# Gated linear attention between two expert layers: outputs in two parts, state copies on ScalarE, factors on GpSimd, a predicated mask, one table set

## The chip, the cores and the metric

The kernel runs on one core of one Trainium2 chip. The metric is the device time of one execution in microseconds, the lower the better; several executions give a median.

## What is computed

A block of three layers over x of 4096 tokens by 256: an expert layer at half weight, an attention layer, and the expert layer again with the same weights. Only the attention layer is touched. Cut to what matters:

```python
def step(S, qkva):                       # for each head, S is 64 x 64
    q_t, k_t, v_t, a_t = qkva
    S = a_t[..., None] * S + k_t[..., None] * v_t[..., None, :]
    o_t = jnp.einsum('bhk,bhkv->bhv', q_t, S)
    return (S, o_t)
# q, k, v = x @ W_q, x @ W_k, x @ W_v in 16 heads of 64; a = sigmoid(x @ W_gate + b_gate)
x = x + 0.5 * _L0_ffn_ref(_layernorm(x, axis=-1), ...)
x = x + _L0_attn_ref(_layernorm(x, axis=-1), W_q, W_k, W_v, W_gate, b_gate, W_o)
x = x + 0.5 * _L0_ffn_ref(_layernorm(x, axis=-1), ...)
```

## The kernel before

Each engine has a program of its own, and every hand-over between engines is a semaphore that the program names. `route` and `expert` are the expert layers; `attention()` on each engine is the stage in between.

**Tiling.** The tokens go in 8 supertiles of 4 tiles of 128 (`NSUP`, `SUPER`), the 16 heads in 8 pairs of two (`NPAIR`), so that a pair's 2 x 64 channels fill 128 partitions. The recurrence is written in chunks of 128 tokens: within a chunk a masked product of keys and queries (`scores`, `mask`), between chunks a state per pair that a scan carries on. Weights are fp32 split in two parts, and each projection (L616, L640, L698) is three passes over them.

**One pair, before the change.** A supertile is a loop body of 8 pairs; 7 supertiles run in a hardware loop and the last one follows it. For pair g of a supertile, with G = 8s + g:

- TensorE projects the gate of pair g+1 (`project_z`), turns the decayed keys (L650), takes the scores (L657), takes the outputs of pair g-1 (L683 from the state, L686 from the masked scores, alternating chunk by chunk), takes the additions to the state (L671, into bank 7), and projects q and k of pair g+1 (`project_qk`, L616).
- ScalarE makes Exp and Ln of the gates (L874, L876), copies the turned keys out of PSUM, makes the two decays with Exp (L883, L885), and rounds the outputs to their high part (`split_o`, by the helper at L757).
- VectorE does `chain` for pair g-1 (spread of the factors L1312, seed of the scan L1314, scan L1315, two spreads of the states into `state_in` L1319, copy-back L1321), sums the logs of pair g+1 (L1269), combines a token tile of the next supertile or takes its statistics, masks the scores (L1298, L1300, four pieces because one quarter of a chunk is never used), scales q and k of pair g+1 (`scaled`, L1277 to L1287, behind which `qk_made` rises), and takes the low part of the outputs of pair g-2 (`split_o`, L1326, behind which `ot_split` rises).
- GpSimd issues the indirect gathers of expert rows (L440), two for each token tile, each as soon as the tile's buffer is free.

**What sets the order.** The order on each engine is written out by hand in `supertile`; an engine waits in its own program order. `qd` is there twice, `prob`, `kd`, `state_in`, `factors`, `states` and each PSUM bank once, so the mask of pair g waits for the outputs of pair g-1 (`o_done`), and the outputs of g-1 wait for the chain of g-1 (`state_ready`) and the split of g-2 (`ot_split`). At the end of a supertile TensorE turns the next x, projects pair 0 of the next supertile, takes the last outputs, waits for their split, makes the output projection (L698) and the next values (`values`, L640, between which ScalarE makes Exp and Ln of the next pair 1), and goes round the loop.

## Time and profile before

| | us |
|---|---|
| median of 3 runs | 2530.24 |
| lowest, highest | 2522.37, 2537.93 |
| span of the profiled execution | 2566.5 |
| TensorE matmul busy in it | 2116.7 (82%) |
| VectorE busy | 1436.0 (56%) |
| ScalarE busy | 1187.6 (46%) |
| GpSimd busy | 263.8 (10%) |

The profiled execution is a single one of its own; of it the span from its first to its last instruction is recorded and no other time. The profile gives for each instruction its start and its duration, and for idle time in front of it what ended that. A matmul's end is modelled, so distances from start to start are the safer reading on TensorE. Matmuls of full fp32 appear as two instructions each.

### The profile page before, as it was taken

The page shows a single profiled execution, that of the slowest core. Times are in us where ns is not written, and L with a number is a line of the kernel's source. Part 1 is how long each engine was busy: PE and PEld are TensorE (multiplying, and loading weights), DVE is VectorE, ACT ScalarE, POOL GpSimd, SP SyncE. Part 2 cuts the span into 40 slices and gives each one's busy share as a digit, 9 for nine tenths or more (in the row PEclk, how much of TensorE's full clock was granted, in tenths as well). Part 3 has the DMA queues.
Part 4 walks back from the last instruction along what each step waited for, and adds up shares of the span by engine and source line. Part 5 has one row for each costly group of instructions (what it writes and reads, how often), then busy time and mean ns, then how long its engine had stood idle before and what let it go on. Part 6 is the DMA issues. An engine that isn't in the chain of part 4 may idle for free.

```text
span 2566.5 us, 39014 instructions
## 1 busy us (share of the span) xinstructions
PE 2116.7 (82%) x13967; PEld 1819.4 (71%) x13968; DVE 1436.0 (56%) x3544; ACT 1187.6 (46%) x1927; POOL 263.8 (10%) x268
## 2 busy tenths in 40 slices
PE   6079999999958897989888888985199999999780
PEld 5069889888856766666666666765088899988670
DVE  6345554555556675848494848556155545555442
ACT  1056655566535363535353544431166555666330
POOL 1700000000021010000000000003600000000324
PEclk9999999999979999989999999985599999999895
DMA  6322222222220000000000000001411221222214
GB/s 240 134 95 91 90 90 74 63 85 72 83 69 17 1 17 5 14 6 14 6 14 10 9 2 1 1 1 52 169 52 66 90 74 49 86 88 70 85 37 131
DMA packets 95432, 151.14 MB, mean 59 GB/s; under 512 B 9583, under 2 KB 76678, under 8 KB 94068
## 3 DMA queue, kind: packets, MB, share of 16 engines
q1 hardware_dynamic: 83008, 116.46, 13.4%
q0 software_dynamic: 12288, 32.91, 4.1%
q8 instruction: 81, 1.33, 0.2%
q14 instruction: 55, 0.45, 0.1%
HBM read 98.84 MB, written 51.15 MB: 58 GB/s over the span
## 4 chain that ended last, share of the span: by engine, by line
PE 55%; DVE 17%; issue 11%; PEld 7%; POOL 3%; ACT 3%; another core or an unknown queue 1%; SPq 1%; DMA 1%; PEldq 1%; DVEq 0%; POOLq 0%; ACTq 0%
PE bank L545 25%; PE bank L564 11%; PE bank L698 4%; PEld bank L564 3%; PEld bank L545 3%; PE bank L683 3%; PE bank L616 3%; PE bank L686 3%; PE bank L640 3%; DVE wide L1298 2%; DVE wide L1315 2%; DVE wide L1287 2%; DVE wide L1300 2%; DVE temp L1319 2%; DVE halves L1326 2%
## 5 line engine op out<-in xcount | busy, mean ns | idle before, releaser
L545 PE MATMUL bank<-halves 128*128 128x512 f32 (+2 forms) x3744 | 778.6, 368 | 35.5 <-DVE halves L1121 22.3
L545 PEld LDWEIGHTS bank<-halves 128*128 128x128 f32 x3744 | 654.0, 192 | 144.3 <-issue 28.3
L564 PE MATMUL bank<-halves 128*128 128x256 f32 (+1 forms) x3288 | 403.1, 283 | 3.0 <-issue 3.0
L564 PEld LDWEIGHTS bank<-halves 128*128 128x128 f32 (+1 forms) x3288 | 397.3, 189 | 5.7 <-issue 4.8
L801 ACT ACTIVATE temp<-bank,bias_now 128x512 f32<-128x512 f32 (+1 forms) x312 | 200.3, 642 | 389.0 <-PE bank L545 369.6
L1134 DVE SCALAR_TENSOR_TENSOR temp<-bank,bias_fc,temp 128x512 f32<-128x512 f32 (+1 forms) x312 | 216.1, 693 | 247.8 <-ACT temp L801 238.9
L616 PE MATMUL bank<-halves 128*128 128x512 f32 x1152 | 292.6, 406 | 2.0 <-DVE halves L1261 2.0
L1141 DVE TENSOR_TENSOR halves<-temp,halves 128x512 fp32r<-128x512 f32 (+1 forms) x312 | 198.1, 635 | 126.8 <-ACT halves L757 122.0
L616 PEld LDWEIGHTS bank<-halves 128*128 128x128 f32 x1152 | 217.0, 194 | 52.1 <-DVE halves L1261 2.4
L440 POOL DMA_INDIRECT halves<-expert_out,read_slot x96 | 102.9, 1072 | 1284.5 <-DMA expert_out<-rows 654.0
L757 ACT ACTIVATE halves<-temp 128x512 fp32r<-128x512 f32 (+1 forms) x313 | 184.9, 591 | 9.9
L1156 DVE TENSOR_TENSOR rows<-bank,rows 128x256 f32<-128x256 f32 (+1 forms) x160 | 66.8, 422 | 217.0 <-PE bank L564 191.0
L757 ACT ACTIVATE halves<-bank 128x512 fp32r<-128x512 f32 (+1 forms) x176 | 90.1, 545 | 211.4 <-PE bank L526 127.4
L808 ACT ACTIVATE temp<-temp 128x512 f32<-128x512 f32 (+1 forms) x312 | 179.9, 576 | 0.2
L683 PE MATMUL bank<-wide,temp 128*128 128x128 f32 x512 | 126.7, 330 | 63.9 <-DVE temp L1319 50.2
L433 POOL DMA_INDIRECT expert_in<-wide,temp x128 | 127.5, 996 | 422.1 <-DVE temp L1047 339.9
L757 ACT ACTIVATE halves<-wide 128x512 fp32r<-128x512 f32 (+1 forms) x196 | 115.5, 644 | 114.5 <-issue 96.5
L683 PEld LDWEIGHTS bank<-wide,temp 128*128 128x128 f32 x512 | 78.4, 193 | 110.1 <-issue 109.2
L1269 DVE TENSOR_TENSOR_SCAN wide<-wide,limit 128x64 f32<-128x64 f32 x512 | 101.0, 269 | 95.9 <-ACT wide L876 90.9
L526 PE MATMUL bank<-ident,wide 128*128 128x128 f32 x320 | 43.4, 276 | 122.6 <-DMA wide<-expert_in 122.6
L1298 DVE TENSOR_TENSOR wide<-bank,causal 64x512 f32<-64x512 f32 x128 | 87.3, 682 | 96.2 <-PE bank L657 54.7
L874 ACT ACTIVATE wide<-bank,bias_gate 128x512 f32<-128x512 f32 x64 | 44.0, 687 | 206.7 <-PE bank L616 183.3
(159 smaller groups left out, 2327.9 us busy)
## 6 DMA issues: line engine op xcount, KB each, us to landing
expert_out<-rows SPq DMA_DIRECT2D x144, 128.0 KB, 1.7
wide<-in_L_ffn_w_c_fc SPq DMA_DIRECT2D x16, 1024.0 KB
wide<-in_L_ffn_w_gate SPq DMA_DIRECT2D x16, 1024.0 KB
wide<-in_L_ffn_w_c_proj SPq DMA_DIRECT2D x16, 1024.0 KB
wide<-expert_in SPq DMA_DIRECT2D x32, 512.0 KB, 4.9
expert_in<-halves SPq DMA_DIRECT2D x9, 1024.0 KB
x<-in_L_attn_x SPq DMA_DIRECT2D x4, 1024.0 KB, 9.5
out_x<-x SPq DMA_DIRECT2D x32, 128.0 KB
```

Of the source, the lines that this page charges most:

```text
L433: pool.indirect_dma_start(expert_in, bass.IndirectOffsetOnAxis(ap=write_slot[:, j:j + 1], axis=0), xn[:, i, :], None, bounds_check=ROWS - ...
L440: pool.indirect_dma_start(into, None, expert_out, bass.IndirectOffsetOnAxis(ap=read_slot[:, j:j + 1], axis=0)).then_inc(landed, 16)
L545: m = pe.matmul(bank[at + b][:, 0:w], a[:, kc, j * P:(j + 1) * P], v[:, kc, 0:w], start=(i == 0), stop=(i == len(ps) - 1))
L564: mm = pe.matmul(bank[4 + t % 2][0:m, 0:C], a[:, j, o:o + m], v[:, j, :], start=(k == 0), stop=(k == len(ps) - 1))
L616: m = pe.matmul(bank[at][:], a[:, kc, g * P:(g + 1) * P], v[:, kc, :], start=(i == 0), stop=(i == len(ps) - 1))
L683: pe.matmul(bank[5][:, cols], state_in[:, c, :], qd[g % 2][:, c, :], start=True, stop=False, skip_group_check=True)
L757: return nc.scalar.activation(o, i, ACT.Copy)
L801: nc.scalar.activation(g_sb[b][:, 0:w], bank[2 + b][:, 0:w], ACT.Identity, bias=bias_now[:, j:j + 1]).then_inc(g_copied, 1)
L808: nc.scalar.activation(hg[b][:, 0:w], hg[b][:, 0:w], ACT.Silu).then_inc(silu_made, 1)
L1134: v.scalar_tensor_tensor(hg[b][:, 0:w], bank[b][:, 0:w], bias_fc[:, bass.ds(col, 1)], g_sb[b][:, 0:w], ALU.add, ALU.mult).then_inc(hg_made, 1)
L1141: v.tensor_tensor(s_lo[buf][:, j, 0:w], hg[b][:, 0:w], as_f32(s_hi[buf][:, j, 0:w]), ALU.subtract).then_inc(s_split, 1)
L1298: v.tensor_tensor(prob[h][lower, :, :], sc[lower, :, :], causal[lower, :].unsqueeze(1).to_broadcast([HALF, SUPER, P]), ALU.mult)
```

## The change

- **TensorE**: `scores` is cut in two, `turn_keys` and `scores`; `outputs` is cut in two, `outputs_of_state` (four products of the state, one behind the other) and `local_outputs` (eight products of the masked scores). For pair g the order is now turn_keys(g), outputs_of_state(g-1), scores(g), local_outputs(g-1), additions(g). `additions` waits for `state_seeded` in place of `state_kept`.
- **ScalarE**: it takes over the seed of the scan (`seed_states`), the two spreads and the copy-back (`spread_states`). One table set that holds Exp and Ln is loaded ahead of the stage.
- **GpSimd**: it takes over the spread of the factors (`spread_factors`), and its gathers are put in its program between these, one tile's in front of each of the first four pairs.
- **VectorE**: `mask` becomes a memset of one element and two predicated copies of whole blocks over buffers cleared once; `chain` is the scan alone, and is done for pair g right behind the mask of g, ahead of the split of g-1 and of `scaled` for g+1.

```diff
+                def spread_factors(s, g):
+                    G = s * NPAIR + g
+                    pool.wait_ge(qk_made, G + 1)
+                    if G:
+                        pool.wait_ge(state_summed, G)
+                    nc.gpsimd.tensor_copy(factors.rearrange("p (n c) -> p n c", n=DH),
+                                          carry[:, g % 2, :].unsqueeze(1).to_broadcast([P, DH, SUPER + 2])
+                                          ).then_inc(factors_made, 1)
...
+                    for b in range(SUPER):
+                        combine_from(b)
+                    for s in range(NSUP):
+                        for g in range(NPAIR):
+                            if s + 1 < NSUP and g < SUPER:
+                                combine_from((s + 1) * SUPER + g)
+                            spread_factors(s, g)
...
+                def outputs_of_state(s, g):
                     G = s * NPAIR + g
-                    pe.wait_ge(prob_made, G + 1)
                     if g:
                         pe.wait_ge(ot_split, G)
                     pe.wait_ge(state_ready, G + 1)
                     for c in range(SUPER):
-                        cols = slice(c * P, (c + 1) * P)
-                        pe.matmul(bank[5][:, cols], state_in[:, c, :], qd[g % 2][:, c, :],
-                                  start=True, stop=False, skip_group_check=True)
+                        pe.matmul(bank[5][:, c * P:(c + 1) * P], state_in[:, c, :], qd[g % 2][:, c, :],
+                                  start=(c == 0), stop=False, skip_group_check=True)
+
+                def local_outputs(s, g):
+                    pe.wait_ge(prob_made, s * NPAIR + g + 1)
+                    for c in range(SUPER):
                         for h in range(2):
-                            m = pe.matmul(bank[5][h * DH:(h + 1) * DH, cols],
+                            m = pe.matmul(bank[5][h * DH:(h + 1) * DH, c * P:(c + 1) * P],
                                           v_sb[:, c, g * P + h * DH:g * P + (h + 1) * DH], prob[h][:, c, :],
-                                          start=False, stop=True, skip_group_check=True)
+                                          start=False, stop=(c == SUPER - 1), skip_group_check=True)
                     m.then_inc(o_done, 1)
...
-                        scores(s, g)
+                        turn_keys(s, g)
                         if g + 1 == NPAIR and not last:
                             turn_x(s + 1)
+                        if g:
+                            outputs_of_state(s, g - 1)
+                        scores(s, g)
                         if g == 0:
                             project_qk(s, 1)
                         else:
-                            outputs(s, g - 1)
+                            local_outputs(s, g - 1)
                         additions(s, g)
...
+                def seed_states(s, g):
+                    G = s * NPAIR + g
+                    if g:
+                        act.wait_ge(state_summed, G)
+                    kv = bank[7][:, 0:DH * (SUPER + 2)].rearrange("p (n c) -> p n c", n=DH)
+                    copy(kv[:, :, 1], state[:, g, :]).then_inc(state_seeded, 1)
+
+                def spread_states(s, g):
+                    act.wait_ge(state_summed, s * NPAIR + g + 1)
+                    st = states.rearrange("p (n c) -> p n c", n=DH)
+                    for h in range(2):
+                        hp = slice(h * DH, (h + 1) * DH)
+                        i = copy(state_in[hp, :, hp].rearrange("p c n -> p n c"), st[hp, :, 1:SUPER + 1])
+                    i.then_inc(state_ready, 1)
+                    copy(state[:, g, :], st[:, :, SUPER + 1]).then_inc(state_kept, 1)
...
                         turned_keys(s, g)
+                        seed_states(s, g)
...
                         if g:
                             split_o(s, g - 1)
+                        spread_states(s, g)
...
+                nc.scalar.preload_act_table_set("natural_log_exp_and_others")
+                act.wait_ge(att_cleared, ATT_CLEARS)
...
-                    v.memset(prob[h][HALF:P, :, 0:HALF], 0.0).then_inc(att_cleared, 1)
+                    v.memset(prob[h], 0.0).then_inc(att_cleared, 1)
...
+                    v.memset(pause[:], 0.0)
                     for h in range(2):
                         sc = bank[3 + h][:].rearrange("p (a n) -> p a n", n=P)
-                        v.tensor_tensor(prob[h][lower, :, :], sc[lower, :, :],
-                                        causal[lower, :].unsqueeze(1).to_broadcast([HALF, SUPER, P]), ALU.mult)
-                        ins = v.tensor_tensor(prob[h][upper, :, upper], sc[upper, :, upper],
-                                              causal[upper, upper].unsqueeze(1).to_broadcast([HALF, SUPER, HALF]),
-                                              ALU.mult)
+                        ins = v.copy_predicated(prob[h], causal[:].bitcast(U16).unsqueeze(1).to_broadcast([P, SUPER, P]), sc)
                     ins.then_inc(prob_made, 1)
...
-                    dve.wait_ge(qk_made, G + 1)
-                    steps.after(v.tensor_copy(f, carry[:, g % 2, :].unsqueeze(1).to_broadcast([P, DH, SUPER + 2])))
+                    dve.wait_ge(factors_made, G + 1)
+                    if g:
+                        dve.wait_ge(state_kept, G)
                     dve.wait_ge(kv_done, G + 1)
-                    steps.after(v.tensor_copy(kv[:, :, 1], state[:, g, :]))
-                    steps.after(v.tensor_tensor_scan(states, bank[7][:, 0:DH * (SUPER + 2)], factors, 0.0,
-                                                     ALU.add, ALU.mult))
-                    for h in range(2):
-                        hp = slice(h * DH, (h + 1) * DH)
-                        ins = v.tensor_copy(state_in[hp, :, hp].rearrange("p c n -> p n c"), st[hp, :, 1:SUPER + 1])
-                    ins.then_inc(state_ready, 1)
-                    v.tensor_copy(state[:, g, :], st[:, :, SUPER + 1]).then_inc(state_kept, 1)
-                    dve.wait_ge(state_kept, G + 1)
+                    v.tensor_tensor_scan(states, bank[7][:, 0:DH * (SUPER + 2)], factors, 0.0,
+                                         ALU.add, ALU.mult).then_inc(state_summed, 1)
...
                     for g in range(NPAIR):
-                        if g:
-                            chain(s, g - 1)
...
                         mask(s, g)
+                        chain(s, g)
+                        if g:
+                            split_o(s, g - 1)
                         if g + 1 < NPAIR:
                             scaled(s, g + 1)
-                            if g:
-                                split_o(s, g - 1)
...
-                    chain(s, NPAIR - 1)
-                    split_o(s, NPAIR - 2)
```

## Rows read from the trace of the kernel before

**Rows 1.** Attention stage: length, busy PE PEld DVE ACT POOL, PEclk, DMA, GB/s
```profile
792.40:1718.50 926.10, 801.82 (x6033) 627.81 (x6033) 628.82 (x1898) 431.39 (x588) 45.38 (x48) 0.96 0.03 8
```

**Rows 2.** Timeline, TensorE, one pair: start, us, engine line operation [idle before]
```profile
1168.40 0.66 PE L650 MATMUL bank<-ident,wide 128*128 128x128 f32 x4
1168.98 1.16 PE L657 MATMUL bank<-wide 64*128 64x128 f32 x16
1171.42 0.46 PE L683 MATMUL bank<-wide,temp 128*128 128x128 f32 x2 [1.28 <-DVE temp L1319]
1171.81 0.44 PE L686 MATMUL bank<-wide 128*64 128x128 f32 x4
...
1174.44 0.64 PE L671 MATMUL bank<-wide,temp 128*64 128x64 f32 x16
...
1179.22 0.60 PE L650 MATMUL bank<-ident,wide 128*128 128x128 f32 x4
```

**Rows 3.** Timeline, VectorE, the same pair
```profile
1168.26 0.68 DVE L1326 TENSOR_TENSOR halves<-bank,halves 128x512 fp32r<-128x512 f32 x1
...
1171.64 1.78 DVE L1269 TENSOR_TENSOR_SCAN wide<-wide,limit 128x64 f32<-128x64 f32 x8
...
1174.73 0.68 DVE L1298 TENSOR_TENSOR wide<-bank,causal 64x512 f32<-64x512 f32 x1
...
1177.02 0.15 DVE L1277 COPY carry<-wide 128x1 f32<-128x1 f32 x1
...
1178.73 0.68 DVE L1326 TENSOR_TENSOR halves<-bank,halves 128x512 fp32r<-128x512 f32 x1
```

**Rows 4.** Chain of waits that ended last, 1168 to 1212 us, shares by line
```profile
by line: DVE wide L1287 10.7%; DVE wide L1298 9.3%; DVE wide L1315 8.8%; PE bank L683 8.5%; PE bank L686 7.7%; PE bank L616 7.6%; DVE temp L1319 7.0%; DVE halves L1326 6.8%; DVE wide L1269 6.6%; issue 6.6%; DVE wide L1300 5.8%; DVE temp L13
```

**Rows 5.** Timeline, TensorE, places in the first and the fifth supertile
```profile
797.05 0.69 PE L671 MATMUL bank<-wide,temp 128*64 128x64 f32 x16
...
799.16 0.60 PE L650 MATMUL bank<-ident,wide 128*128 128x128 f32 x4
...
1270.48 1.12 PE L650 MATMUL bank<-ident,wide 128*128 128x128 f32 x4 [5.28 <-issue]
...
1280.07 0.60 PE L650 MATMUL bank<-ident,wide 128*128 128x128 f32 x4
...
1343.07 0.66 PE L650 MATMUL bank<-ident,wide 128*128 128x128 f32 x4 [0.85 <-DVE wide L1287]
...
1344.74 1.09 PE L610 MATMUL bank<-ident,rows 128*128 128x128 f32 x8
...
1355.23 0.46 PE L683 MATMUL bank<-wide,temp 128*128 128x128 f32 x2 [1.15 <-DVE halves L1326]
...
1359.84 11.78 PE L698 MATMUL bank<-halves 128*128 128x256 f32 x96 [1.42 <-DVE halves L1326]
...
1383.50 1.65 PE L640 MATMUL bank<-halves 128*128 128x512 f32 x6 [0.97 <-ACT wide L757]
```

**Rows 6.** Groups by line: line engine op xcount | busy us, mean ns | idle before
```profile
L876 ACT ACT_TABLE_LOAD x64 | 82.1, 1283 | 1.2
L757 ACT ACTIVATE temp<-bank 128x512 f32<-128x512 f32 x80 | 46.0, 586 | 98.7 <-PE bank L650 77.2 <-PE bank L487 13.0 <-remote 8.5
L1315 DVE TENSOR_TENSOR_SCAN wide<-bank,temp 128x384 f32<-128x384 f32 x64 | 61.2, 956 | 2.2
L1300 DVE TENSOR_TENSOR wide<-bank,causal 64x256 f32<-64x256 f32 x128 | 54.7, 428 | 1.8
```

**Rows 7.** Groups by line, GpSimd
```profile
L416 POOL TENSOR_SCALAR_AFFINE_SELECT ident<-ident 128x128 f32<-128x128 f32 x1 | 0.3, 288 | 0.2 <-POOL before L415 0.2
```

**Rows 8.** Timeline, TensorE, last supertile
```profile
1637.88 0.60 PE L650 MATMUL bank<-ident,wide 128*128 128x128 f32 x4
...
1699.43 0.66 PE L650 MATMUL bank<-ident,wide 128*128 128x128 f32 x4 [0.85 <-DVE wide L1287]
...
1718.46 14.12 PE L698 MATMUL bank<-halves 128*128 128x256 f32 x96 [1.42 <-DVE halves L1326]
```

34 lines of the change are left out of this document (18 added, 16 removed).

## The prediction

> **What bounds the kernel.** I read the table by stretches first: of the span, 926 us lie between the first score of the attention stage and its last head pair, TensorE busy for 802 of them and VectorE for 629 [rows 1]. Every line of the diff lies in this stage, so only there can time go or come. Within it I read the timeline of one head pair. TensorE's work fills 9.54 us (from the key transpose at L650 to the next one, 10.82 us, less 1.28 us of waiting in front of the state outputs, L683) [rows 2]. VectorE's loop closes in 10.47 us: from one split of the outputs (L1326, 1168.26) to the next (1178.73) [rows 3]. The six pairs in the middle of a supertile take 63.0 us from the first one's transpose to the last pair's (1280.07 to 1343.07), 10.5 each [rows 5]. So neither engine is full: what sets the pace is a loop between them. In it stand, one behind the other: the split and the chain of a pair (factors, seed, scan, two spreads: 1168.26 to 1171.42), the outputs on TensorE (to 1174.44, then 0.29 until the mask at 1174.73), four mask pieces (to 1177.02), and carry and scaled q and k (to the next split, 1178.73). 3.16 + 3.02 + 0.29 + 2.29 + 1.71 = 10.47 [rows 2, 3]. The trace's chain of waits names the same members, none over 11% [rows 4].
>
> **The change, step by step.** Let t be the start of a pair's key transpose.
>
> *Tables.* Two loads of 1.283 us go from each of 64 pairs, 164 us of ScalarE [rows 6]. On the path of a pair they cost nothing now: ScalarE waits. What they cost is seen in the values stage, where one holds a copy back and TensorE waits 0.97 us [rows 5]: 0.97 less in each of 8 values stages, and some 0.3 more in the first. One more load lies alone on the way to the first normalisation: 1.3. In front of the loop this makes 2.6. That all of them go I take from the order of functions: Exp, Ln and copies are all that the stage runs, and the copies get no load of their own now. Trainium skill ("ScalarE: Activation LUTs", What ACT_TABLE_LOAD costs): a switch is the load and a drain, 2.66 us. By that the nine exposed loads would give some 12 us more than my sum, 2440. The trace shows 1.283 us a load, and the wait it causes is 0.97, so the rows decide.
>
> *Work moved off VectorE.* The factors go to POOL; the seed, two spreads and the copy-back to ScalarE. Of the 3.16 us only the split, 0.6 to the next start, and the scan, 0.956, stay [rows 6]. POOL shows no copy. Below it is bounded by 0.29 us for 128 elements [rows 7], above by three of these, 0.9. I take 0.9. It has from t to the scan, over 5 us, so it is hidden; it would show from 5 us on. Its queue also holds the gathers of a later tile, issued about one pair ahead of the combine that wants them, where before they were issued a supertile ahead; a pair of them is some 2.5 us, and they fit. Trainium skill ("GPSIMD Engine Reference", Engine selection) puts elementwise work on VectorE, since POOL is some twice slower with two inputs. Even at twice my 0.9 the sum would not move. ScalarE's four small copies cost more than nothing and at most 0.59 each, what one of 128x512 takes [rows 6]: at most 2.4 us a pair, under the 2.57 that the table loads give up. For 256 elements I take 0.40, for 64 0.24: 1.3 us a pair. The seed runs right behind the key copy, before the additions need it. The spread of pair g now has until pair g+1's state outputs, more than 2 us: hidden. Queued behind it is only the next pair's first Exp, whose matmul ends later.
>
> *Mask.* Two 512-element and two 256-element pieces (0.68 and 0.43 each, 2.29 us in all to the carry) become a one-element memset (0.07, the step at which the one-element carry copies follow each other) and two masked copies of 128x512 [rows 3, 6]. No masked copy is in the trace. Below: 0.68, the full-rate PSUM read of the same size. Above: 1.2, twice the element time that 0.68 for 512 against 0.43 for 256 gives (1 ns each). I take 0.68, since a mask and a source are two inputs, as the multiply has. With 0.07 it makes 1.45, 0.84 less than now.
>
> *Outputs in two parts.* Now four groups alternate, each two state matmuls (0.39 until the next form starts) and four local ones, 3.02 / 4 = 0.76 a group [rows 2]. Transposes that follow each other in one form need 1.09 for 8, 0.12 to 0.13 each [rows 5]; the scores need 1.16 for 16, 0.07 each [rows 2]. So the alternation itself seems to cost: 2 x 0.12 and 4 x 0.07 are 0.52, not 0.76. Below: parts in a row, 8 x 0.12 = 0.94 and 16 x 0.07 = 1.09, with two more changes of form at 0.13: 2.3 us instead of 3.02. Above: nothing is gained, 3.02. I take 2.3, a gain of 0.72 to 0.75 (0.75 below), as the rows of all other groups in one form say so; the other end is a rival.
>
> *The new loop.* t + 0.58 transpose + state outputs with their change of form 1.07 + scores 1.09 + local outputs 1.23 = 3.97; + 0.28 to the mask; + 1.45; scan 1.0; split 0.6; carry and scaled 1.80 (1.71 and the overlap of the next); 0.06 to TensorE: 9.16 us. TensorE's own work becomes 9.54 - 0.75 = 8.8, still less. VectorE must also have summed the logs (L1269, from about t + 1.5, when Ln ends) and combined a tile: from L1269's start to the mask 3.09 us without a gap [rows 3], so the mask could start at t + 4.6 at worst where 4.25 is wanted, and the variance pair is longer; I charge 1.2 us a supertile. Six pairs: 6 x 9.16 + 1.2 = 56.2 against 63.0: -6.8.
>
> *First pair, a loss.* It has no outputs. At present the second transpose starts 2.1 us after the additions, 797.05 to 799.16 [rows 5]. With the change the scan stands in front of the scaling of pair 1, and it waits for those additions: 0.6 + 0.28 + 1.0 + 1.8 + 0.06 = 3.7 instead of 2.1: +1.6.
>
> *Last pair of a supertile.* From its transpose to the output projection 16.77 us (1343.07 to 1359.84) [rows 5]. Two outputs are 0.75 shorter each. The wait for the split of pair 6, 1.15 [rows 5], goes, since that split now ends before the next projections do, and with it a short one for the state, some 0.3: -2.9.
>
> *Sum.* A supertile: -6.8 + 1.6 - 2.9 - 0.97 = -9.1; seven: -64. The last: 61.6 (1637.88 to 1699.43) to 55 in its pairs, +1.6, and its end, 19.03 us from transpose to projection [rows 8], where nothing covers VectorE: 4.25 + 1.45 + 1.0 to the scan's end, 0.8 spread, 3.2 outputs (TensorE at its lower level doubles part of it, as now), 1.5 split: 12.2 to 13: -6.5. Together -11.5. In front: -2.6. All: -78 us, on a profiled execution whose span is 2566.5. The runs' median is 2530.2, 36 less, and a difference within this stage should carry over: 2452 us.
>
> What does not change: five of the loop's turns begin with TensorE idle, with the reason "issue", the one shown for 5.28 us, after which small transposes take twice their time, 1.12 against 0.60: the lower level, 1.2 GHz. TensorE's code for a turn is as long as before.
>
> **Rivals.**
> *The split gives nothing* (outputs 3.02): the loop is 9.91, 3.6 us a supertile in the pairs, 1.45 at its end; a supertile -4.4, the last -5, all -38: 2492. For it: the ends of matmuls are modelled. Against: the one-form rows. 20%.
> *Masked copies at two cycles an element*, 1.2 each: + 1.04 x 62 pairs: 2516, within 1%. 8%.
> *Masked copies that read mask, source and old value one after the other*, three cycles, 1.75 each: + 2.1 x 62 = +133: 2585, slower. It decides from 0.68 + 78/124 = 1.3 us a copy (no gain) and 1.5 (1% slower). For it: a masked copy must keep what the mask leaves out. Against: the slowest streaming row, the scan, is at 2.1 ns an element. 5%.
> *The table loads stay*: Ln ends 1.28 later, sum, combine and mask follow at t + 5.6, the loop is 10.5 as now; only the ends gain: about 2514. 4%.
> *More than forecast*: local matmuls at 0.05 apart as inside their groups of four, fewer drops of the clock: 2432. 12%.
> *A new drop of TensorE's clock* in the first pair's longer wait, or slower code supply: +3 us each for such a pair (estimated as a third of a turn's first pair, 1270.48 to 1280.07, that runs mostly at the lower level [rows 5]), 2475 to 2560. 6%.
>
> **Numbers.** The forecast has 45%, own range 2430 to 2475. Range for 8 in 10: 2425 to 2505, which takes in the forecast, the useless split and the larger gain. About 1% is what a measurement of this kernel can tell from no change. Faster by over 1% (under 2505): 0.79. Within 1%: 0.12. Slower: 0.09.
>
> **What would show it.** No table load in the stage. A masked copy of 0.68. Eight state matmuls in a row in about 1.07, local ones in 1.1 to 1.25, and no wait in front of the state outputs. Key transposes 9.2 us apart in the pairs, 8.3 from first to second. TensorE idle in front of the transpose, released by the scaling of q and k. Wrong if the mask starts late behind the combine, if the masked copy is over 1 us, or if POOL's factors end after the additions.

## The result, and the profile after

| | median, us | lowest to highest | span of the profiled execution |
|---|---|---|---|
| kernel before | 2532.0 | 2522.4 to 2537.9 | 2566.5 |
| changed kernel | 2387.5 | 2385.0 to 2395.1 | 2384.2 |

The ratio is 0.944, 95% interval 0.940 to 0.948. The change takes 144.5 us off, where 78 were forecast: the forecast is right in sign, has little more than half of the gain, and the time lies outside its range. Of all executions behind this document one was slow, 3571 us at a granted clock of 0.55 for the kernel with the chain back on VectorE; no median has it in.

The attention stage, of the changed kernel, and one head pair in it (length, busy time of PE, PEld, DVE, ACT and POOL, PEclk, DMA share, GB/s):

```profile
786.84:1570.14 783.30, 712.86 (x6033) 606.85 (x6033) 456.06 (x1514) 379.17 (x719) 81.77 (x115) 0.98 0.04 10
1114.50:1123.10 8.60, 8.43 (x79) 7.06 (x79) 6.99 (x23) 5.34 (x10) 2.42 (x3) 1.00 0.10 30
```

Against [rows 1] the stage is 142.8 us shorter: nearly all of the gain lies in it. TensorE issues the same 6033 instructions and is busy 89 us less: the same matmuls, in another order, take less time, and some of it is the clock, granted at 0.98 for 0.96. VectorE is busy 173 us less. In the pair shown TensorE is busy for 8.43 of 8.60 us; before, it was 9.54 of 10.82 [rows 2].

That pair on TensorE:

```profile
1114.50 0.66 PE L671 MATMUL bank<-ident,wide 128*128 128x128 f32 x4 [0.16 <-DVE wide L1343]
1115.00 1.06 PE L708 MATMUL bank<-wide,temp 128*128 128x128 f32 x8
1115.98 1.16 PE L682 MATMUL bank<-wide 64*128 64x128 f32 x16
1117.07 1.09 PE L716 MATMUL bank<-wide 128*64 128x128 f32 x16
1118.00 0.63 PE L695 MATMUL bank<-wide,temp 128*64 128x64 f32 x16
1118.56 4.37 PE L638 MATMUL bank<-halves 128*128 128x512 f32 x18
1123.10 0.66 PE L671 MATMUL bank<-ident,wide 128*128 128x128 f32 x4 [0.16 <-DVE wide L1343]
```

and on VectorE:

```profile
1115.92 1.58 DVE L1325 TENSOR_TENSOR_SCAN wide<-wide,limit 128x64 f32<-128x64 f32 x8 [1.48 <-ACT wide L909]
...
1117.75 1.07 DVE L1250 SCALAR_TENSOR_TENSOR x<-halves,weight,x 128x256 f32 x2
1118.75 0.74 DVE L1355 COPY_PREDICATED wide<-causal,bank 128x512 f32<-128x512 uint16 x1
...
1119.38 0.72 DVE L1355 COPY_PREDICATED wide<-causal,bank 128x512 f32<-128x512 uint16 x1
1120.00 0.94 DVE L1366 TENSOR_TENSOR_SCAN wide<-bank,temp 128x384 f32<-128x384 f32 x1
1120.86 0.67 DVE L1371 TENSOR_TENSOR halves<-bank,halves 128x512 fp32r<-128x512 f32 x1
```

The outputs take 0.98 (state, L708) and 0.93 us (local, L716) from start to start, 1.91 in all, where the alternating ones of [rows 2] took 3.02. The wait of 1.28 us in front of the state outputs [rows 2] is gone. A masked copy lasts 0.72 to 0.74 us, and the next instruction starts 0.62 to 0.63 after it. The pair is 8.60 us and not 8.21, because the mask starts late, at t + 4.25, without a gap behind the combine (L1250), and TensorE then waits 0.16. The forecast had named this as a sign of being wrong. VectorE itself starts late in the pair: its sum of the logs waits 1.48 us for Ln (L909 on ScalarE), and Ln stands behind an Exp that waits for the scaling of q and k (L1343):

```profile
1114.54 0.69 ACT L907 ACTIVATE wide<-bank,bias_gate 128x512 f32<-128x512 f32 x1 [0.46 <-DVE wide L1343]
```

GpSimd's spread of the factors, and ScalarE's seed and spreads:

```profile
1114.52 0.50 POOL L465 COPY temp<-carry 128x384 f32<-128x384 f32 x1 [5.71 <-DVE wide L1343]
```

```profile
1116.28 0.22 ACT L790 ACTIVATE bank<-temp 128x64 f32<-128x64 f32 x1
...
1120.98 1.71 ACT L790 ACTIVATE temp<-wide 64x256 f32<-64x256 f32 x3 [1.65 <-DVE wide L1366]
```

Both are hidden, as forecast. Where nothing is combined, the loop through VectorE alone can be read. The changed kernel's last supertile, TensorE and then VectorE; the last of the six middle pairs, in front of which TensorE has fewer projections to make:

```profile
1549.17 0.60 PE L671 MATMUL bank<-ident,wide 128*128 128x128 f32 x4
...
1557.29 0.66 PE L671 MATMUL bank<-ident,wide 128*128 128x128 f32 x4 [1.10 <-DVE wide L1343]
```

```profile
1552.93 0.75 DVE L1355 COPY_PREDICATED wide<-causal,bank 128x512 f32<-128x512 uint16 x1 [0.61 <-PE bank L716]
...
1554.18 0.95 DVE L1366 TENSOR_TENSOR_SCAN wide<-bank,temp 128x384 f32<-128x384 f32 x1
1555.04 0.67 DVE L1371 TENSOR_TENSOR halves<-bank,halves 128x512 fp32r<-128x512 f32 x1
```

The loop: 3.76 us to the mask, 1.25 to the scan, 0.86 to the split, 2.25 through split, carry and scaling to the next transpose, 8.12 in all. In the other pairs of this supertile TensorE does not wait and they last 8.21: its own work is now as long as the loop.

All 64 pairs by the start of their key transposes, summed over the eight supertiles (from TensorE's timelines, us):

| | before | after | difference | forecast |
|---|---|---|---|---|
| first pair to second | 63.4 | 74.7 | +11.2 | +12.8 |
| six middle pairs | 512.8 | 411.3 | -101.5 | -54 |
| last pair to the output projection | 136.5 | 101.4 | -35.1 | -26.8 |
| output projection to the next supertile | 213.3 | 195.9 | -17.4 | -6.8 |
| of that, idle stretches with the reason "issue" | 33.1 (5) | 26.0 (5) | -7.1 | 0 |

A turn is the way from a supertile's output projection round TensorE's loop to the next supertile. In both profiles five of the seven turns end with TensorE idle for 4.9 to 7.2 us in front of the next key transpose; this is the idle stretch that is counted below.

### The profile page after: what moved, and what is told of

It is laid out like the page before. It is cut to its first block, busy times and chain, and to the rows that moved or that the text cites. A ratio compares the mean times of both kernels' runs of the same rounds, so it can differ in the third digit from the quotient of the medians.

```text
span 2384.2 us, 38690 instructions
## 1 busy us (share of the span) xinstructions
PE 2025.1 (85%) x13967; PEld 1799.6 (75%) x13968; DVE 1263.0 (53%) x3160; ACT 1130.6 (47%) x2054; POOL 298.3 (13%) x332
## 4 chain that ended last, share of the span: by engine, by line
PE 66%; DVE 11%; PEld 7%; issue 6%; POOL 6%; ACT 2%; DMA 1%; PEldq 1%; DVEq 0%; POOLq 0%; SPq 0%; ACTq 0%
PE bank L567 27%; PE bank L586 12%; PE bank L638 5%; PE bank L728 4%; PEld bank L586 4%; POOL expert_in L436 4%; PE bank L662 4%; PEld bank L567 3%; PE bank L682 2%; DVE wide L1343 2%; PE bank L716 2%; POOL halves L443 2%; PE bank L531 2%; PE bank L708 2%; DVE wide L1366 1%
## 5 line engine op out<-in xcount | busy, mean ns | idle before, releaser
L567 PE MATMUL bank<-halves 128*128 128x512 f32 (+2 forms) x3744 | 770.4, 366 | 22.3 <-DVE halves L1177 22.3
L790 ACT ACTIVATE temp<-wide 64x256 f32<-64x256 f32 (+1 forms) x192 | 105.9, 551 | 130.7 <-DVE wide L1366 128.4
L548 PEld LDWEIGHTS bank<-ident,wide 128*128 128x128 f32 x320 | 38.0, 144 | 129.7 <-DMA wide<-expert_in 126.0
L1165 DVE TENSOR_TENSOR halves<-wide,halves 128x512 fp32r<-128x512 f32 x128 | 81.8, 685 | 86.2 <-ACT halves L790 78.1
L465 POOL COPY temp<-carry 128x384 f32<-128x384 f32 x64 | 32.3, 505 | 704.0 <-DVE wide L1343 704.0
```

The source lines that it names most:

```text
L567: m = pe.matmul(bank[at + b][:, 0:w], a[:, kc, j * P:(j + 1) * P], v[:, kc, 0:w], start=(i == 0), stop=(i == len(ps) - 1))
L790: return nc.scalar.activation(o, i, ACT.Copy)
```

## Experiments

No kernel here leaves work out. Pair lengths are distances between key transposes of middle pairs, from each kernel's own timeline. Each ratio is to the kernel before, executed beside the run; its median there is 2530 to 2537 us.

### One part of the change undone

**Alternating outputs** (the changed kernel's order, the two output parts again chunk by chunk at the place of the local ones):

```diff
-                                  start=(c == 0), stop=False, skip_group_check=True)
-
-                def local_outputs(s, g):
-
-                    pe.wait_ge(prob_made, s * NPAIR + g + 1)
-                    for c in range(SUPER):
+                                  start=True, stop=False, skip_group_check=True)
```

> The changed kernel with the outputs in one part again, state and local products alternating chunk by chunk, at the place of the local ones. Theory 'grouping' (the alternation costs TensorE over 1 us a pair): TensorE's work in a pair goes from 8.2 back to about 9.5 us and bounds it; six middle pairs 57 us instead of 51.7, the last pair of a supertile 15 instead of 12.65, some 64 us in all: 2450. Rival 'VectorE' (the gain came from the shorter VectorE part of the loop, and the grouping is worth what the record forecast, 0.75 a pair): the pair is 8.8 to 8.9, six pairs 53.5, in all under 30 us: 2410 to 2415.

Measured: 2448.6 us, ratio 0.964 (0.959 to 0.969). A pair is 9.46 us instead of 8.21 in the last supertile, without a wait of TensorE's. So the grouping of the outputs is worth 1.25 us a pair, and TensorE alone would hold the pair at 9.46. The forecast had 0.75.

**Multiplied mask** (four multiplies in place of memset and two predicated copies):

```diff
-                        ins = v.copy_predicated(prob[h], causal[:].bitcast(U16).unsqueeze(1).to_broadcast([P, SUPER, P]), sc)
+                        v.tensor_tensor(prob[h][lower, :, :], sc[lower, :, :],
+                                        causal[lower, :].unsqueeze(1).to_broadcast([HALF, SUPER, P]), ALU.mult)
...
```

> The changed kernel with the mask as four multiplies again (2.3 us from the first to the carry instead of 1.26 for two predicated copies). Theory 'loop' (mask, scan, split and scaling all lie on the loop that sets a pair): +1.03 a pair where the loop binds now, less 0.1 to 0.4 where TensorE binds; six pairs 57 us, nothing in the first and last pair: +40 to +50 us, 2430 to 2436. Rival (TensorE's order is all that counts): within 10 us of the changed kernel.

Measured: 2419.2 us, ratio 0.955 (0.949 to 0.960). Pairs with a combine 9.64 (8.60 with the predicated copies), without 9.19 (8.21). The price of 1.0 us a pair came as expected. The time is 11 us below the least that was expected; the profiled execution, 2421 us, has the idle stretch at one of its seven turns where the changed kernel's has it at five. The last pairs, for which nothing was expected, are longer too (13.1 to 14.8 us against 12.65). The stage is 818.7 us; less the idle stretches, and less what the first pairs behind them take too long, it is 809 against 746, so that the mask is worth 63 us and not 32.

**The chain back on VectorE** (factors, seed, spreads and copy-back there, in the new order):

```diff
-                            spread_factors(s, g)
...
-                        seed_states(s, g)
...
-                        spread_states(s, g)
...
+                    steps.after(v.tensor_copy(f, carry[:, g % 2, :].unsqueeze(1).to_broadcast([P, DH, SUPER + 2])))
...
+                    steps.after(v.tensor_copy(kv[:, :, 1], state[:, g, :]))
...
+                        ins = v.tensor_copy(state_in[hp, :, hp].rearrange("p c n -> p n c"), st[hp, :, 1:SUPER + 1])
```

> The changed kernel with factors, seed, spreads and copy-back on VectorE again, at their new place behind the mask and ahead of the scaling. Theory 'loop': 1.65 us more of VectorE on the loop of every pair; six middle pairs 51.7 + 9 to 10, first pair +1.6: +80 to +90 us, 2470 to 2480. Rival (these copies are hidden wherever they run, only their wait in front of the outputs counted): under 30 us more.

Measured: 2508.9 us, ratio 0.991 (0.987 to 0.994): some 30 us more than expected. A pair with a combine is 10.47 us. VectorE:

```profile
1164.94 1.57 DVE L1323 TENSOR_TENSOR_SCAN wide<-wide,limit 128x64 f32<-128x64 f32 x8 [1.48 <-ACT wide L910]
...
1167.75 0.74 DVE L1353 COPY_PREDICATED wide<-causal,bank 128x512 f32<-128x512 uint16 x1
...
1168.99 0.35 DVE L1363 COPY temp<-carry 128x384 f32<-128x384 f32 x1
...
1172.52 1.41 DVE L1341 TENSOR_TENSOR wide<-bank,wide 128x256 f32<-128x256 f32 x4
```

From the end of Ln to the scaling there is no gap: sum of the logs, statistics, combine, mask, chain, split, scaling. That is a third loop, closed through ScalarE's Exp and Ln, which wait for the scaling. With the chain in it, it is 10.47 us; without, 8.60. The expectation had left it out.

**Two table sets**:

```diff
-                nc.scalar.preload_act_table_set("natural_log_exp_and_others")
```

> The changed kernel without the one table set, so that Exp and Ln load a table each for every pair again. The record priced the loads at 0.97 a supertile and 2.6 in front while VectorE's fill is not in the way, and at the whole gain if they stay. Theory 'fill' (VectorE sums logs and combines a tile between Ln and the mask, and in three pairs of eight the mask already waits for that): Ln 1.28 later goes straight into pairs two to five and partly into the others; six pairs 57 to 60 us: +45 to +65, 2430 to 2455. Rival 'hidden' (ScalarE has slack): +8 to +15 us, 2395 to 2403.

Measured: 2438.2 us, ratio 0.962 (0.954 to 0.970). Pairs with a combine 9.85 against 8.60, without 8.66 against 8.21. VectorE and ScalarE of that kernel:

```profile
1121.67 1.57 DVE L1324 TENSOR_TENSOR_SCAN wide<-wide,limit 128x64 f32<-128x64 f32 x8 [2.76 <-ACT wide L909]
```

```profile
1119.71 1.28 ACT L909 ACT_TABLE_LOAD   x1
1121.01 0.63 ACT L909 ACTIVATE wide<-wide 128x512 f32<-128x512 f32 x1
```

VectorE waits 2.76 us for the logs in place of 1.48: the whole load, 1.28 us, lies in the third loop. No turn of this kernel's profiled execution ends with an idle stretch. Against the changed kernel with TensorE's program written out (below), which has none either, its stage is 817.9 us to 748.8: the one set is worth 69 us in the new order, more than the 51 of the medians.

The four prices by the medians, 61, 32, 121 and 51 us, add to 265, nearly twice the gain of 144.5. By the stage of each profile, less idle stretches and slow first pairs as above, they are 64, 63, 130 and 72, and the gain is 137. So the parts don't stand beside each other; each needs others.

### One part alone in the kernel before

**The kernel before, again**, for the size of what belongs to one execution.

> The kernel before, unchanged, for a second profile. The first one's span was 36 us over the runs' median, and its pairs showed extra lengths of 1.5 and 3.0 us in places where TensorE ran at its lower level. If these belong to the kernel, they come again, at the same pairs; if they belong to that execution, the span is near 2530 and they are elsewhere or gone.

Measured: 2545.9 us, stage 935.4 us. The middle pairs of 10.47 came again; the longer ones (12.0 to 14.0 us; 10 us too much in the first profile, 18 in this one) came in part in other places: five in the first, seven in this one, three of them at the same pair (the last middle one of the first, third and sixth supertile). So they belong to the kernel, and neither their number nor all their places do. With them go drops of TensorE's clock. One of them in the kernel before, window and TensorE:

```profile
1087.59:1101.52 13.93, 11.31 (x74) 8.16 (x72) 10.20 (x35) 6.23 (x8) 0.00 (x0) 0.75 0.01 1
```

```profile
1091.06 0.46 PE L683 MATMUL bank<-wide,temp 128*128 128x128 f32 x2 [1.77 <-DVE temp L1319]
...
1095.32 1.07 PE L671 MATMUL bank<-wide,temp 128*64 128x64 f32 x16
```

The granted clock is 0.75 of the full 2.4 GHz over the pair; behind the wait of 1.77 us the additions take 1.07 us where they take 0.64 in [rows 2].

**Outputs in two parts**, grouped where the alternating ones stood:

```diff
-                                  start=True, stop=False, skip_group_check=True)
+                                  start=(c == 0), stop=False, skip_group_check=True)
+                    for c in range(SUPER):
+                        cols = slice(c * P, (c + 1) * P)
...
-                                          start=False, stop=True, skip_group_check=True)
+                                          start=False, stop=(c == SUPER - 1), skip_group_check=True)
```

> The kernel before with one edit: the four state products of a pair one behind the other, then the eight local ones, at the old place. Theory 'grouping' (1.1 us of 3.02 a pair go with the alternation): a pair of 10.48 becomes 9.4, both outputs at a supertile's end are shorter too; 64 x 1.1 = 70 us: about 2460. As forecast on record (0.75): 48 us, 2484. Rival (starts in the trace are modelled, nothing is gained): 2532.

Measured: 2484.2 us, ratio 0.981 (0.976 to 0.986). The full 1.04 us a pair shows only where VectorE combines nothing (9.43); pairs with a combine fall from 10.47 to 10.1 or 10.3. VectorE there, sum of the logs to the first mask piece:

```profile
1153.65 1.78 DVE L1271 TENSOR_TENSOR_SCAN wide<-wide,limit 128x64 f32<-128x64 f32 x8
1155.35 0.40 DVE L1241 BATCH_NORM_STATS2 wide<-x 128x6 f32 x1
1155.67 1.07 DVE L1196 SCALAR_TENSOR_TENSOR x<-halves,weight,x 128x256 f32 x2
1156.67 0.67 DVE L1300 TENSOR_TENSOR wide<-bank,causal 64x512 f32<-64x512 f32 x1
```

None of them waits: VectorE is full, 10.1 us of work in a pair. In the kernel before itself VectorE is busy for 9.79 of the 10.47 us from one first mask piece to the next (its busy time in this window of the kernel before is the third):

```profile
1174.73:1185.20 10.47, 9.49 (x84) 7.30 (x82) 9.79 (x30) 6.21 (x10) 1.89 (x2) 1.00 0.09 27
```

**One table set:**

```diff
+                nc.scalar.preload_act_table_set("natural_log_exp_and_others")
```

> The kernel before with one edit: one table set for Exp and Ln, loaded ahead of the stage. By the record: 0.97 in each of seven supertiles and 2.6 in front, 9 to 10 us: 2522. Rival: VectorE's loop of 10.47 holds the log sums and the combine with no gap, so an earlier Ln gives nothing more; more than 20 us would say that the waits for ScalarE in the pairs counted.

Measured: 2514.6 us, ratio 0.990 (0.988 to 0.993). That is 20.6 us under the kernel before beside it, twice what was expected. Most middle pairs are 10.47, as before, so the loads are hidden in them, as the forecast had it. The gain is at the ends (a turn without idle stretch 24.8 us, 26.0 to 26.2 with two sets) and in the first two middle pairs (9.46 and 10.46 to 10.52 us, 9.72 and 10.82 to 10.86 before, some 0.6 a supertile).

**The predicated mask.**

```diff
-                        v.tensor_tensor(prob[h][lower, :, :], sc[lower, :, :],
-                                        causal[lower, :].unsqueeze(1).to_broadcast([HALF, SUPER, P]), ALU.mult)
...
+                        ins = v.copy_predicated(prob[h], causal[:].bitcast(U16).unsqueeze(1).to_broadcast([P, SUPER, P]), sc)
```

> The kernel before with one edit: the mask as a one-element memset and two predicated copies. Theory 'loop': the mask is on the loop of 10.48, and becomes 1.03 shorter by the starts in the changed kernel's trace (0.84 by the record): 7 pairs x 8 x 1.0 less what TensorE's own 9.54 allows (0.94 a pair): 45 to 52 us, 2480 to 2487. Rival: nothing, because something else waits at the same place: within 10 us.

Measured: 2513.4 us, ratio 0.990 (0.987 to 0.994), and the middle pairs are 10.47 us still, although the mask is 1.0 us shorter. The expectation fell, and with it the reading that one loop sets the pace. TensorE and then VectorE of this kernel:

```profile
1170.20 0.46 PE L685 MATMUL bank<-wide,temp 128*128 128x128 f32 x2 [0.98 <-DVE temp L1318]
...
1173.22 0.64 PE L673 MATMUL bank<-wide,temp 128*64 128x64 f32 x16
1173.79 4.38 PE L618 MATMUL bank<-halves 128*128 128x512 f32 x18
...
1180.67 0.46 PE L685 MATMUL bank<-wide,temp 128*128 128x128 f32 x2 [0.98 <-DVE temp L1318]
```

```profile
1176.84 0.76 DVE L1289 TENSOR_TENSOR wide<-bank,wide 128x256 f32<-128x256 f32 x2 [0.61 <-PE bank L618]
1177.51 0.68 DVE L1325 TENSOR_TENSOR halves<-bank,halves 128x512 fp32r<-128x512 f32 x1
1178.11 0.35 DVE L1311 COPY temp<-carry 128x384 f32<-128x384 f32 x1
```

A second loop, in which the mask has no part: outputs 3.02, additions 0.57, projections until the keys can be scaled 3.05, scaling 0.67, split 0.60, chain 2.56 to the next outputs: 10.47. In the kernel before, both loops are 10.47 us long, so whoever shortens one gains nothing.

**Two parts alone, then three.** The kernel before with grouped outputs and predicated mask; the same with the one table set.

> The kernel before with two edits: the outputs in two parts and the predicated mask. If two loops of equal length hold the pairs of the kernel before (the one through the mask and the scan, and one through the queries', keys' projections, the split and the outputs, both 10.47 us) and behind them VectorE's own work (10.1 to 10.3 us in a pair with a combine), the outputs in two parts shorten both loops by about 1.05 us and the mask only the first and VectorE's own work by about 0.85: a pair with a combine falls from 10.47 to about 9.4, the six middle pairs of a supertile to about 57 us, the last pair to about 13.7; in all about 2466 us. Rival, VectorE's own work is no bound: pairs as in the run with the outputs alone, 10.1, and about 2484 us.

> As the run before, with one table set as well: nothing moves to another engine and nothing changes its place. By the loops: the table set gives 9 to 15 us outside the pairs and nothing in them, about 2455 us, so that some 70 us of the change's gain come from the moved steps and their order alone. Rival, the three arithmetic edits carry the change: near its 2387 us.

Measured: 2436.4 us, ratio 0.962 (0.956 to 0.969), and 2409.4 us, ratio 0.949 (0.943 to 0.955). Most middle pairs are 9.43 to 9.49 us in both, combine or not, with the first one at 8.4 to 8.6 and one or two a supertile at 9.8 to 11.5: what the second loop gives with outputs 1.04 us shorter, and not VectorE's fill (10.1). Jointly the two give 94 us where 51 and 22 are the single gains, and the three 121 where the singles add to 93. But both are faster than expected, 2436 for 2466 and 2409 for 2455; where these 30 and 46 us come from isn't taken apart. So the expectation of the three falls too: with every step in its old place and order, these three edits bring most of the whole, five sixths by the medians.

### The new order and the moved steps, apart

**The new order with all the old parts** (alternating outputs, multiplied mask, chain on VectorE, two sets), and **the moved steps in the old order** (scan of pair g-1 at the start of pair g, scores ahead of the outputs, the three arithmetic edits kept):

> The change's order of work on TensorE and VectorE, but with the old parts: outputs alternating in one part, the mask multiplied, the chain of state steps on VectorE, two table sets. The loop through transpose 0.58, scores 1.09, outputs 3.02, 0.28 to the mask, mask 2.29, scan and chain 2.55, split 0.6 and scaled 1.8 is then one loop of about 12.2 us a pair, against 10.47: slower than the kernel before, about 2600 to 2630 us. Rival, the order itself brings the gain: below 2500 us.

> The three arithmetic edits and the moved steps (factors on GpSimd; seed, spreads, copy-back on ScalarE), but the old order: scan of pair g-1 at the start of pair g, scores ahead of both outputs. If a loop of split, scan, spread, outputs, additions, projections and scaling sets the pairs of the run with the arithmetic edits alone (9.44 us, TensorE waiting 0.98 for the spread states), the moved steps give nothing here: ScalarE has the spread ready no sooner than VectorE had (scan about 0.95 and two spreads of some 0.7, against factors, seed, scan and spreads in 2.4 us), pairs 9.3 to 9.5, in all 2400 to 2420 us. Then the moved steps are worth something only together with the new order, which alone costs some 100 us. Rival, the moved steps pay in any order: near the changed kernel's 2387 us or below, since the first pair loses nothing here.

Measured: 2711.5 us, ratio 1.070 (1.064 to 1.076), and 2452.3 us, ratio 0.968 (0.962 to 0.975). The order alone is 182 us slower than the kernel before: one loop of 13.8 us. TensorE waits for the scaling in it, and works for some 3 us of a pair at its lower level of 1.2 GHz. TensorE of that kernel:

```profile
1282.39 1.12 PE L670 MATMUL bank<-ident,wide 128*128 128x128 f32 x4 [2.62 <-DVE wide L1340]
```

and two windows, one from this line to the end of the scores, one a pair of the last supertile that has no drop of the clock:

```profile
1282.39:1285.45 3.06, 3.06 (x20) 2.50 (x21) 0.35 (x2) 2.99 (x5) 0.00 (x0) 0.50 0.02 5
1801.17:1813.46 12.29, 9.67 (x78) 7.24 (x78) 8.53 (x26) 6.12 (x8) 0.00 (x0) 1.00 0.00 0
```

The granted clock is 0.50 in the first. Transposes and scores take 3.06 us where they take 1.67 at full clock (0.58 and 1.09), 1.4 more a pair: that, with the 12.2 expected, makes 13.6 of the 13.8. Of the 48 middle pairs 41 last 13.65 to 13.85 us at a granted clock of 0.87 or 0.88, three 15.1 to 15.9 at 0.58 to 0.66, and the four at full clock 12.3 (without a combine) and 12.8 (with one).

In the old order the moved steps are a loss against the same kernel with the chain on VectorE, and the time is 32 us over the most that was expected. ScalarE, then VectorE:

```profile
1160.04 1.64 ACT L789 ACTIVATE temp<-wide 64x256 f32<-64x256 f32 x3 [3.77 <-DVE wide L1367]
1161.58 0.67 ACT L906 ACTIVATE wide<-bank,bias_gate 128x512 f32<-128x512 f32 x1
```

```profile
1162.95 1.57 DVE L1326 TENSOR_TENSOR_SCAN wide<-wide,limit 128x64 f32<-128x64 f32 x8 [2.94 <-ACT wide L908]
```

The spreads stand in front of Exp and Ln on ScalarE, so the sum of the logs starts late and VectorE waits 2.94 us; the middle pairs behind the first are 9.9 to 10.5 us. Another place for the spreads in ScalarE's program wasn't tried. The square, with the three arithmetic edits in all four:

| median, us | chain on VectorE | steps moved |
|---|---|---|
| old order | 2409.4 | 2452.3 |
| new order | 2508.9 | 2387.5 |

By the medians the moved steps alone cost 43 us, the new order alone costs 99, and both together gain 22. This 22 isn't clear of the noise: the ratios are 0.949 (0.943 to 0.955) and 0.944 (0.940 to 0.948). Part of the differences is the turns of the loop: three ended idle in the profile at 2409, six in that at 2452, five in the changed kernel's. The stage of each profile, without these stretches and without what first pairs behind them take too long:

| stage in the pairs' own time, us | chain on VectorE | steps moved |
|---|---|---|
| old order | 815.0 - 18.9 - 6.6 = 789.5 | 850.3 - 35.2 - 13.6 = 801.5 |
| new order | 908.5 - 25.1 - 7.7 = 875.7 | 783.3 - 26.0 - 11.1 = 746.2 |

(The kernel before: 926.1 - 33.1 - 9.4 = 883.6.) The signs stay, each from one profile: moved steps alone +12, new order alone +86, both -43, and the three edits in place -94 of the whole -137.

### The order once more, and the loop's turns

**First pair**: the additions ahead of the projections of pair 1. **State outputs first**: also the state outputs ahead of the key transposes, and on VectorE statistics and combine ahead of the sum of the logs:

```diff
+                        if g:
+                            outputs_of_state(s, g - 1)
                         turn_keys(s, g)
-                        if g:
-                            outputs_of_state(s, g - 1)
                         scores(s, g)
...
-                        if g + 1 < NPAIR:
-                            sum_logs(s, g + 1)
...
+                        if g + 1 < NPAIR:
+                            sum_logs(s, g + 1)
```

> The changed kernel with one edit: in the first pair of a supertile TensorE takes the additions to the state before it projects q and k of pair 1, so that the scan need not wait for that projection. Theory 'first pair' (its 1.2 us are the price of the scan standing in front of the scaling and waiting for late additions): first pair 6.8 instead of 7.95 us, 8 x 1.2 = 9 us, 2378. Rival (the scaling waits for k anyway, or the scan is late for another reason): no change within 3 us.

> The kernel with the additions first, and two more edits: VectorE takes statistics and combine before the log sums (they need no Ln, and fill the 1.5 us in which it waits for ScalarE), and TensorE takes the state outputs of a pair before it turns the next pair's keys. Theory 'fill' (the 8.6 us pairs are VectorE full between Ln and mask, the 9.0 one the variances, and the transpose waits for the scaling with nothing to do): all pairs near TensorE's own 8.25, pair seven's wait of 1.66 shorter by 1.0; six pairs 49.5 instead of 51.7; with the first pair 25 us in all: 2360. Rival: the log sums come too late for the decays and the scaling waits for these, six pairs stay at 51.7 or more.

Measured: 2374.9 us, ratio 0.937 (0.931 to 0.943), and 2349.0 us, ratio 0.929 (0.923 to 0.935). The first pair, without an idle stretch before it, is 6.51 us instead of 7.95. With the state outputs first all middle pairs but the last are 8.21 us, combine or not, and TensorE has no gap in them:

```profile
1109.14 1.05 PE L708 MATMUL bank<-wide,temp 128*128 128x128 f32 x8
1110.03 0.60 PE L671 MATMUL bank<-ident,wide 128*128 128x128 f32 x4
...
1117.36 1.05 PE L708 MATMUL bank<-wide,temp 128*128 128x128 f32 x8
```

VectorE's wait for Ln in the third loop, 1.48 us before, is now used for the combine (0.29 is left of it in such a pair), and TensorE's own work is the bound that is left. Three edits stand in this kernel, and what each gives isn't taken apart.

**TensorE's program written out** for seven supertiles instead of a hardware loop, in the changed kernel and in the one with the state outputs first:

```diff
-                with pe.Fori(0, NSUP - 1) as s:
+                for s in range(NSUP - 1):
```

> The changed kernel with one edit: TensorE's program for the first seven supertiles is written out instead of a hardware loop; the other engines keep theirs. Theory 'code' (the 5 us of idle with the reason issue at a turn's start is TensorE's program being fetched again behind the branch; the profiles so far show 36 packets on instruction queue 8 and 9 more for each such idle stretch, and the lower level of the clock follows it): no such stretch, first pairs 7.95, five times 6.5 us less: 2355. Rival (TensorE stands for another reason at that place, or straight code is fetched no faster): the stretches stay, 2385.

> Additions first, log sums last, state outputs first, and TensorE's program written out: if both theories hold their gains add, 25 + 33 us: about 2330. If the code theory falls, this is equal to the kernel without the last edit, about 2360.

Measured: 2349.1 us, ratio 0.928 (0.922 to 0.934), and 2318.9 us, ratio 0.917 (0.911 to 0.922), the fastest kernel here, 69 us under the changed one. Every turn now takes 24.80 us from the output projection to the next transposes, with 0.7 us idle before them and first pairs of 7.93 and 7.37 us.

## Why the prediction was right in sign and half in size

The median is 64.5 us under the forecast. In the profiles the stage gained 142.8 us where the forecast had 75 for it; the 68 between them are made up as follows, by the table of stretches above.

**The new loop, 9.16 us: 8.21 measured, 45.6 us over 48 pairs.** This is the step that failed most. The members were named rightly: transpose, state outputs, scores, local outputs, mask, scan, split, carry and scaling. Their lengths, from start to start, forecast and measured: outputs 1.07 + 1.23 against 0.98 + 0.93 (0.39 too long), transpose 0.58 against 0.49, mask 1.45 against 1.26, scan 1.0 against 0.86, carry and scaled with the 0.06 behind them 1.86 against 1.65: together 1.0. TensorE's own work, forecast at 8.8, is 8.21, a little more than the 8.12 of this loop. The largest is *Outputs in two parts*: gain 0.75 forecast, with nothing as the far end. I took 0.12 a matmul from transposes, and a change of form at 0.13; the runs with the outputs alternated and grouped show 1.04 to 1.25 us. Most of the rest is one habit: a new VectorE term was taken as a duration, where the next instruction starts before the last one ends (0.62 for copies of 0.72).

**"I charge 1.2 us a supertile": 2.5 measured, 9 us the other way.** The six middle pairs of the first seven supertiles take 51.7 us, and 49.3 in the last, where nothing is combined. The forecast had the mask wanted at t + 4.25 and VectorE ready for it by t + 4.6 at worst. VectorE was ready at 4.25, but with TensorE faster than forecast the mask was wanted at 3.76. VectorE's readiness is the third loop, through Exp and Ln, which the forecast mentions as work to be done and not as a loop.

**The clock in the kernel before, 10 us.** 63.0 us was taken for each six pairs; the profiled execution has 512.8 in all where eight undisturbed ones make 502.6. The rest is in the pairs with a lower clock. They stand in other places in the repeated run, and none is in the middle pairs of the changed kernel's profile, although TensorE waits up to 1.7 us in front of one pair of a supertile there too. What decides whether the clock drops behind such a wait isn't shown.

**Last pair, -35.1 for -26.8, 8 us.** Two outputs are 1.1 shorter each, not 0.75, and the wait for the split of pair 6 went, as forecast; that is 16.77 to 12.65 us. Of the 4.1 us some 0.8 are not taken apart.

**Values and turn, -17.4 for -6.8, 11 us.** The table load in the values stage went (0.97 forecast; the turn is 1.2 to 1.4 us shorter with one set in the runs with and without it). 7 us are idle stretches of 4.9 to 5.6 us each in place of 5.3 to 7.2; why they are shorter isn't shown. The first pair, +1.2 us for +1.6, was right but for 1.6 us in all.

**"So neither engine is full: what sets the pace is a loop between them."** Half wrong, and the sum hid it. The share by stretches, VectorE 629 of 926 us [rows 1], is a mean over pairs, values and output projection; in a pair with a combine VectorE is busy 9.79 of 10.47, and there are a second loop of the same 10.47 and its own 10.1 to 10.3 us of work. Had the change been the mask alone, the forecast's method would have promised 0.84 us a pair and got nothing in the pairs of 10.47. It came out right in sign because the change shortens all of them at once. [rows 4] had said so: no member above 11%, and in the list the projections (L616, 7.6%), which have no place in the loop that I summed.

**"On the path of a pair they cost nothing now."** Nearly true in the kernel before (10.47 with one set and with two; some 0.6 us a supertile in the first two middle pairs), but it doesn't carry over to the new kernel: there the load in front of Ln would lie in the third loop, at 1.28 us a pair. The forecast never asked what the removed load would cost in the new loop; it needed the answer only for the rival *The table loads stay*, which it put at 2514. The run with two sets gives 2438. The Trainium skill ("ScalarE: Activation LUTs", What ACT_TABLE_LOAD costs) has 2.66 us for a switch with its drain; here a load is 1.28 us, the activation behind it starts 0.02 us after its end, and VectorE's wait grows by 1.28, so of a drain the trace shows nothing, and the trace decides.

**What was right**: no table load in the stage, the masked copies near 0.7 us (of the rivals with two and three cycles an element nothing is left), GpSimd's copy hidden (0.50 us on GpSimd, 0.35 on VectorE), and the loss in the first pair. The Trainium skill ("GPSIMD Engine Reference", Engine selection) puts elementwise work on VectorE, GpSimd being some twice slower with two inputs and roughly at line rate with one; for this copy the ratio is 1.4. GpSimd's copy was moved only together with ScalarE's, and the square of four runs says of them all that the move pays only with the new order. That the five idle stretches stayed five was luck: the profiles here have from none to six, and the kernel with the multiplied mask, in which TensorE's program is unchanged, has one.

**What the change is worth by parts** can't be told as a sum. Taken out singly its parts cost 265 us, put in singly three of them give 93, and the fourth with its order is worth 22 by the medians (43 by the stage), out of two losses. Two tied loops and a nearly full engine must be shortened together.

## What to carry to other kernels

Before pricing an edit, list every loop that closes through the stage and the work of each engine in the busiest kind of iteration, and ask of each edit which of them it does not shorten; a pace that two of them share makes single edits look worthless and joint ones cheap. Price new terms from start to start, never by their durations, and judge an order together with the steps moved for it, since either half alone may be a large loss. Issue matmuls of one form behind each other where their order is free, and write a long loop body out if its turns end with idle time.

## What the hardware showed that I had not expected

**Alternating forms.** Matmuls of a 128 x 128 stationary operand and of 128 x 64, in turn, took 3.02 us for the eight and sixteen instructions; the same in two groups took 1.91 to 1.98 us. What costs in the alternation isn't shown: besides the change of form, each local output there adds to the block that the state output in front of it has just written, and the `start` and `stop` marks differ; no run has one of these without the others.

**A loop's turn.** Of the seven turns, none to six end with TensorE idle for 4.8 to 7.3 us, with the reason "issue". The queue of kind "instruction" carries 9 packets for each such stretch and 36 without any. This fits all sixteen profiles of kernels with TensorE's loop. The changed kernel (five stretches), the one with two table sets (none) and the one with the state outputs first (six):

```profile
q8 instruction: 81, 1.33, 0.2%
```

```profile
q8 instruction: 36, 0.59, 0.1%
```

```profile
q8 instruction: 90, 1.47, 0.3%
```

In the changed kernel a packet of this queue starts at 1298.0 and the next one at 1301.5, and the idle stretch is from 1298.5 to 1304.07; with two table sets the queue has none from 871 to 1536 us. So TensorE waits for its own code. Behind the stretch it works at 1.2 GHz for a while; the changed kernel, with a granted clock of 0.50 from 1304.07 to 1307.12:

```profile
1304.07 1.11 PE L671 MATMUL bank<-ident,wide 128*128 128x128 f32 x4 [5.55 <-issue]
1305.11 2.08 PE L682 MATMUL bank<-wide 64*128 64x128 f32 x16
```

The first pair is then 9.5 to 10.8 us instead of 7.95. Written out, the program has none of the stretches, with 73 packets in all, and 38 us come back (30 in the kernel with the state outputs first). What decides whether a turn finds its code ready isn't known; the two profiles of the kernel before have five stretches each, four of them at the same turns and one at another.

**Idle time that lowers the clock.** In the kernel with the new order alone TensorE waits 2.6 us in nearly every pair, and 44 of the 48 middle pairs have a stretch at the lower level somewhere: pairs at a mean granted clock of 0.87 last 13.7 us where one at full clock lasts 12.3. So an idle engine lengthens the very loop that it waits in, by 1.4 us. Where in the pair the drop falls differs: in the last supertile the transposes right behind a wait of 2.6 us still run at full clock (0.66 us). What decides it isn't shown.
